# A Mamba block between two ternary feed-forward halves: fifteen states of the second token half by ScalarE and accumulating DMAs, other pieces moved, loops written out

## The reference, cut to what matters

```python
x = x + 0.5 * ffn(layernorm(x))          # ffn: x @ (ternary(W) * scale).T + bias
x = x + mamba(layernorm(x))
x = x + 0.5 * ffn(layernorm(x))

# mamba: u, z = split(x @ W_in.T); u = silu(causal conv over 4 tokens)
#        dt, B, C from u @ W_xproj.T; dt = softplus(dt @ W_dt.T + b_dt)
# for each of 16 states n, along all 4096 tokens:
h[n] = exp(dt * A[n]) * h[n] + dt * B[n] * u
y   += C[n] * h[n]
# then y = (y + u * Dskip) * silu(z); result y @ W_out.T
```

## Time and profile before

| what | us |
|---|---|
| median of 3 runs (2982.8 to 2990.77) | 2988.41 |
| the profiled execution, its own time | 2993.49 |
| its span, first to last instruction | 2991.6 |
| busy over the span: TensorE (82%) | 2457.8 |
| VectorE (83%) | 2483.3 |
| ScalarE (65%) | 1943.3 |
| GpSimd (64%) | 1921.5 |

### The profile page before, as it was taken

One profiled execution on the slowest core, in us unless ns is written; L12 is line 12 of the kernel. 1 busy time (PEld: TensorE's weight loads), 2 busy tenths in 40 slices (PEclk: granted clock), 3 DMA queues, 4 the chain that ended last, 5 costly groups with the idle time before them and its releaser, 6 DMA issues.

```text
span 2991.6 us, 42858 instructions
## 1 busy us (share of the span) xinstructions
PE 2457.8 (82%) x12448; PEld 1413.9 (47%) x12448; DVE 2483.3 (83%) x3261; ACT 1943.3 (65%) x3457; POOL 1921.5 (64%) x1705
## 2 busy tenths in 40 slices
PE   3577999899998726788889888888888888889887
PEld 1233444444443315555555555555555555555553
DVE  5565666767666649999999999999999999999991
ACT  2233766756765666677777767767777767777772
POOL 1112222222221138899989989989989989999983
PEclk8788999999998857799999999999999999999998
DMA  5454233233232263352352352353352352343330
GB/s 206 155 205 168 78 128 135 78 128 121 92 128 107 79 214 117 92 131 69 112 132 68 99 140 74 99 132 82 98 133 76 102 135 72 106 119 87 105 76 35
DMA packets 175016, 337.66 MB, mean 113 GB/s; under 512 B 41696, under 2 KB 91104, under 8 KB 174496
## 3 DMA queue, kind: packets, MB, share of 16 engines
q1 hardware_dynamic: 160928, 284.23, 28.8%
q0 software_dynamic: 13824, 50.34, 8.8%
HBM read 174.61 MB, written 109.58 MB: 95 GB/s over the span
## 4 chain that ended last, share of the span: by engine, by line
POOL 28%; DVE 13%; issue 12%; PE 5%; DMA 3%; ACT 1%; POOLq 1%; SPq 0%; DVEq 0%; ACTq 0%
POOL dbu L1055 22%; DVE h L1279 9%; DVE y L1292 3%; PE p_g L1402 2%; PE p_g L1411 1%; PE p_ht L1368 1%; POOL o L1100 1%; DMA y<-y_part 1%; POOL carry L1066 1%; POOL y L1075 1%; POOL y L1090 1%; POOL x L1094 1%; DMA dt_<-dt_scratch 1%; POOL dbu L1060 1%; DMA dtu_<-dtu_scratch 1%
## 5 line engine op out<-in xcount | busy, mean ns | idle before, releaser
L1279 DVE TENSOR_TENSOR_SCAN h<-p_da,dbu 128x512 f32<-128x512 f32 x1024 | 1189.0, 1206 | 44.7 <-ACT p_da L1161 21.9
L1055 POOL TENSOR_TENSOR dbu<-dtu_,bb 128x1024 f32<-128x1024 f32 x512 | 1205.3, 2385 | 4.7 <-DMA dtu_<-dtu_scratch 4.1
L1161 ACT ACTIVATE p_da<-dt_,neg_a 128x255 f32<-128x255 f32 x2048 | 886.5, 467 | 400.3 <-DVE h L1279 377.5
L1368 PE MATMUL p_ht<-ident,h 128*128 128x128 f32 x4096 | 596.6, 305 | 157.9 <-DVE h L1279 156.7
L1368 PEld LDWEIGHTS p_ht<-ident,h 128*128 128x128 f32 x4096 | 534.6, 159 | 250.5 <-issue 111.2
L1292 DVE SCALAR_TENSOR_TENSOR y<-p_ht,ct,y 128x1024 f32<-128x1024 f32 x400 | 505.9, 1265 | 4.9 <-PE p_ht L1368 4.8
L714 PE MATMUL p_u<-xz,wu 128*128 128x512 f16 x1536 | 351.4, 386 | 10.8 <-DVE xz L508 9.2
L1402 PE MATMUL p_g<-wo,tokt 128*128 128x512 f16 x1536 | 355.2, 389 | 1.6 <-ACT tokt L1193 1.6
L70 POOL TENSOR_TENSOR small<-small,consts 128x1 f32<-128x1 f32 x96 | 71.1, 740 | 441.4 <-DVE small L63 441.4
L1411 PE MATMUL p_g<-wz,xz 128*128 128x512 f16 x1536 | 345.2, 381 | 0.0
L363 POOL TENSOR_TENSOR late<-dt,u 128x512 f32<-128x512 f32 x64 | 81.7, 1276 | 378.0 <-DVE dt L561 378.0
(11 more groups left out here) (120 smaller groups left out, 3053.7 us busy)
## 6 DMA issues: line engine op xcount, KB each, us to landing
y<-y_part POOLq DMA_DIRECT2D x96, 512.0 KB, 5.8
bb<-b_scratch SPq DMA_DIRECT2D x128, 256.0 KB, 3.5
xin<-in_x SPq DMA_DIRECT2D x32, 512.0 KB, 5.5
x_scratch<-x SPq DMA_DIRECT2D x32, 512.0 KB, 4.8
xz_scratch<-xz SPq DMA_DIRECT2D x16, 1024.0 KB, 6.0
y_scratch<-late SPq DMA_DIRECT2D x32, 512.0 KB, 5.1
dt_scratch<-dt SPq DMA_DIRECT2D x64, 256.0 KB, 2.1
dtu_scratch<-late SPq DMA_DIRECT2D x64, 256.0 KB, 2.4
```

The lines of the kernel that those rows point to most:

```text
L1055: nc.gpsimd.tensor_tensor(state[:, 4 * f:4 * f + 4, :], dtu[:, 4 * f:4 * f + 4, :], bb[n // NB % 2][:, n % NB:n % NB + 1, :].to_broadcast( ...
L1161: ins_ = nc.scalar.activation(p_da[p % 2][:, k * T2 + 1:(k + 1) * T2], dt[:, g, 1:], ACT.Exp, scale=neg_a[:, g, n:n + 1])
L1279: nc.vector.tensor_tensor_scan(h[n % 2][:, 2 * p:2 * p + 2, :].rearrange("p g t -> p (g t)"), p_da[p % 2][:], dbu[n % 2][:, 2 * p:2 * p + ...
L1368: mm = nc.tensor.transpose(p_ht[t][:, g * P:(g + 1) * P], h[n % 2][:, g, t * P:(t + 1) * P], ident[:])
```

## The change

State parts. All states but 0 of the token half t = 1 are now written by ScalarE. State 2 goes directly to the one `y2`, the 14 others to one of three `y_part` tiles, from which GpSimd's accumulating DMAs add them three slots later: the odd ones to y itself, the even ones to y2. y2 is added to y by one more accumulating DMA.

```diff
-        y2 = [sb(f"y2_{i}", [P, D]) for i in range(2)]
-        part = [sb(f"y2_part{i}", [P, D]) for i in range(2)]
+        y2 = sb("y2", [P, D])
+        part = [sb(f"y_part{i}", [P, D]) for i in range(3)]
...
-        PARTED = (0, 5, 7, 8, 10, 11, 12)
-        SUMS = len(PARTED) - 1
+        PARTED = tuple(range(1, NS))
+        Y2_FIRST, MERGE = 2, NS
+        Y_SUM, Y2_SUM = (1, 3, 5, 7, 9, 11, 13, MERGE, 15), (4, 6, 8, 10, 12, 14)
+        SUMMED = tuple(n for n in PARTED if n != Y2_FIRST)
...
-                def add_part(c, cpar, k):
-                    wait(pool, y_added[1], c * NS + PARTED[k] + 1)
-                    wait(pool, part_added, (c * SUMS + k - 1) * 16)
-                    nc.gpsimd.tensor_tensor(small[:, 44:45], consts["minus_half"], consts["minus_half"], ALU.mult
-                                            ).then_inc(part_ready, 1)
-                    pool.wait_ge(part_ready, 1)
-                    pool.dma_start(y2[cpar][:], part[k % 2][:], accum_op=ALU.add).then_inc(part_added, 16)
+                def add_part(c, cpar, n):
+                    into, sums, done = (y[cpar][1], Y_SUM, y_summed[cpar]) if n in Y_SUM else (y2, Y2_SUM, y2_summed)
+                    wait(pool, y_added[1], c * NS + n + 1)
+                    if sums.index(n):
+                        wait(pool, *summed(c, sums[sums.index(n) - 1]))
+                    pool.dma_start(into[:], part[part_of(c, n) % 3][:], accum_op=ALU.add).then_inc(done, 16)
...
-                    nc.gpsimd.tensor_tensor(y[cpar][1][:], y[cpar][1][:], y2[cpar][:], ALU.add).then_inc(merged, 1)
+                    pool.dma_start(y[cpar][1][:], y2[:], accum_op=ALU.add).then_inc(y_summed[cpar], 16)
```

```diff
-                    nc.gpsimd.tensor_tensor(x1[t][:], x1[t][:], half_bias[:], ALU.add).then_inc(xb_done, 1)
+                    pool.dma_start(x1[t][:], dram["hb"], accum_op=ALU.add).then_inc(xb_done[t], 16)
...
+                def finish(c, t, x):
...
+                    nc.vector.scalar_tensor_tensor(out=o[x][:], in0=p_g[b][:], scalar=consts["ffn_scale"],
+                                                   in1=x1[t][:, x * HALF:(x + 1) * HALF],
                                                    op0=ALU.mult, op1=ALU.add).then_inc(g_free[b], 1)
```

Places. The units are spread anew, one slot each (a pair of `t` or `n` halves counts as one), with the last z of a chunk in slot 1 of the next body:

```diff
-        FFN = {0: [("f", 1, 0)], 1: [("f", 1, 1)]}
-        OUT = {4: [("t", 0, 0), ("t", 0, 1)], 5: [("o", 0, 0)], 6: [("o", 0, 1)], 7: [("t", 1, 0), ("t", 1, 1)],
-               8: [("o", 1, 0)], 9: [("o", 1, 1)], 10: [("n", 0, 0), ("n", 0, 1)], 13: [("f", 0, 0)],
-               14: [("f", 0, 1)], 15: [("n", 1, 0), ("n", 1, 1)]}
-        ZED = {2: [("z", 0, 0)], 3: [("z", 0, 1)], 11: [("z", 1, 0)], 12: [("z", 1, 1)]}
+        LAST = {0: [("n", 1, 0), ("n", 1, 1)], 2: [("f", 1, 0)], 3: [("f", 1, 1)]}
+        OUT = {1: [("z", 1, 1)], 4: [("t", 0, 0), ("t", 0, 1)], 6: [("o", 0, 0)], 7: [("o", 0, 1)],
+               8: [("t", 1, 0), ("t", 1, 1)], 10: [("o", 1, 0)], 11: [("o", 1, 1)], 12: [("n", 0, 0), ("n", 0, 1)],
+               14: [("f", 0, 0)], 15: [("f", 0, 1)]}
+        ZED = {5: [("z", 0, 0)], 9: [("z", 0, 1)], 13: [("z", 1, 0)]}
```

GpSimd (c_on: work for chunk i-1):

```diff
-                            if n - 3 in PARTED[1:]:
-                                add_part(i, par, PARTED.index(n - 3))
-                        if e_on:
-                            if n == 1:
-                                finish(i - 1, i - 2, 0, 1)
-                            if n == 5:
-                                add_bias(i - 2, 1)
-                            if n in (6, 7):
-                                finish(i, i - 2, 1, n - 6)
+                            if n - 3 in SUMMED:
+                                add_part(i, par, n - 3)
+                        if e_on and n == 1:
+                            add_bias(i - 2, 1)
                         if c_on:
-                            if n == 3:
+                            if n in (0, 1, 3):
+                                add_part(i - 1, 1 - par, {0: 13, 1: 14, 3: 15}[n])
+                            if n in (2, 6):
+                                gate(i - 1, 1 - par, n // 6)
+                            if n == 2:
                                 merge(i - 1, 1 - par)
-                            if n in (2, 4):
-                                gate(i - 1, 1 - par, n // 4)
```

The row scales are made in slots 10 and 14 (13 before), the first bias in 13 (12). On ScalarE tanh stands in slots 2, 6, 10 and 14 (3, 4, 12 and 13), the absolute means in 2 and 6 (2 and 4), `scale_y` in 3 and 7 (3 and 5), `high` in 0, 4, 8 and 12, `normalise` in 11 and 15; `low` takes its first half behind the first two pairs of decays of the slot after, and its second behind the other two. On VectorE:

```diff
+                            if n in (6, 10, 14):
+                                silu_part(i, n // 14, n % 6 // 4)
+                        if c_on and n == 2:
+                            silu_part(c, 1, 1)
+                        if c_on and n in (3, 7):
+                            token_scale(c, 1 - par, n // 7)
                         add_state_before(i, par, n, 0)
-                        if c_on and n in (7, 10):
-                            add_product(i, n // 10, 1)
+                        if c_on and n in (7, 8, 11, 12):
+                            add_product(c, n // 11, (n - 7) % 4)
+                        if c_on and n in (8, 12):
...
+                            row_stats(dve, nc, x1[t], stats, mv, vn, small[:, 40:41], ln_chain, stats_ready,
+                                      scale_ready, c * TT2 + t)
+                        if c_on and n == 15:
+                            finish(c, 0, 0)
+                        if e_on and n == 0:
+                            finish(i - 2, 0, 1)
+                        if e_on and n in (3, 4):
+                            finish(i - 2, 1, n - 3)
```

Loops. Both `drive` functions have no loop any more:

```diff
-            body(0, 0)
-            body(1, 1)
-            with eng.Fori(0, (C2 - 4) // 2) as turn:
-                body(turn * 2 + 2, 0)
-                body(turn * 2 + 3, 1)
-            for i in range(C2 - 2, C2 + 2):
+            for i in range(C2 + 2):
                 body(i, i % 2)
```

296 lines of the change are left out of this document (145 added, 151 removed).

## The result

The changed kernel takes **3041.1 us**, median of 4 runs (3038.7 to 3045.8), against 2989.6 of the kernel before on the same chip: a ratio of 1.0179, 95% interval 1.0158 to 1.0199. It is 1.8% slower, where the forecast was 1.7% faster. Its profiled execution has a span of 3040.7 us, 49.1 more than before.

What follows compares the result with a forecast made beforehand. VectorE was taken as the bound, slot by slot. A chunk of 110.3 us against 113.4 saves 46.5 us, the first chunk 7.0, loops 3, and the tail costs 5: 51.5 us saved, 2937 us, range 2857 to 3005.

Steps and rivals of the forecast that it cites:

- VectorE 104.1: Per chunk of the second pass: VectorE's busy time falls from 110.9 to 104.1 us, eight additions going and four finish operations coming.
- GpSimd 101.7: Per chunk: GpSimd's busy time falls from 105.5 to 101.7 us, with 11 more DMA issues at 0.90 us, 9.9 in all.
- its cover: GpSimd's products run about a slot ahead of the scans, hiding its issues while GpSimd is below VectorE, by 2.4 us.
- GpSimd busy over 107 a chunk, from issues dearer than 0.90: Sign in the changed profile that would show the forecast wrong altogether; GpSimd was expected busy 100 to 102 us.
- The merge, whose landing the prediction put only in the tail, as hidden: After the last chunk: the last sums and merge, three landings in a row, 17 us, hidden behind transposes and o units.
- TensorE 4.8 us late in three places: Per chunk: TensorE makes VectorE wait 1.7 us at slot 8, 2.3 over slots 9 to 11, 0.8 in slot 14.
- Rival 2: TensorE's units after gaps start at the lower clock, some 1 us in three places: chunk 113.3, 2982 us; chance 0.13.
- rival 1: VectorE alone is the bound, TensorE's clock stays up and it is never late: chunk 105.1, 2857 us; chance 0.25.
- First chunk, 7.0 saved: First chunk of the second pass, with none of the later work: 7.0 us saved from 105.3, bounds 9.4 and 4.
- Loops, 3 us and the rest inside 113.4: First pass's one jump back saves 3 us; second pass's jumps are already inside the 113.4 us chunk; straight code costs nothing.
- The tail, +5: After the last chunk's scans: the z unit of its second half now comes there, about 5 us more on the path.
- Rival 3: Sums land late and ScalarE waits: a loss from landings of 10.1 us; at 11 us, chunk 116.6, 3031 us; chance 0.14.

Runs made afterwards that it cites:

- a_small: Changed kernel with all part sums and the merge issued, each adding only 8 of 1,024 columns: 3005.3 us, ratio 1.0056.
- a_nosum: Changed kernel without the fourteen part sums and the merge of each chunk, ScalarE's part states kept: 2964.4 us, ratio 0.9924.
- a_8rows: Changed kernel with every part sum and the merge over only 8 of 128 partitions, whole rows: 2993.7 us, ratio 1.0018.
- a_sum14: Changed kernel with the sum of state 14 issued one slot earlier, in slot 0: 3017.6 us, ratio 1.0108.
- a_y2: Changed kernel with two y2 tiles, sums of states 13, 14, 15 in slots 0, 1, 2 and the merge in slot 4: 3011.1 us, ratio 1.0074.
- b_noloop: Kernel before the change with both loops written out, nothing else changed: 2964.2 us, ratio 0.9926.
- a_y2_warm: a_y2 with 8 further transposes on TensorE in each slot of turning units: 2996.3 us, ratio 1.0027.
- a_nosum_warm: a_nosum with 8 further transposes on TensorE in each slot of turning units: 2934.1 us, ratio 0.9820.

## Why the prediction was wrong

- **VectorE 104.1:** 105.3. The additions are as counted (272, and 240 parts on ScalarE); the price from start-to-start times was 1.2 too low, I take it because with more pauses fewer instructions overlap their neighbours, which was not tested apart.
- **GpSimd 101.7, "11 more at 0.90", and its cover:** the failed step. The busy time was right: 102.6, at 0.90 an issue. But an issue holds the queue 1.14 us, for 0.28 ahead of it and the products behind it were left out. And the cover was judged by the sum over a chunk ("as long as GpSimd is below VectorE"), where it fails slot by slot: the two dbu buffers let GpSimd run only about a slot ahead, and around the gates of slots 2 and 6 it takes 8.5 to 8.8 us and more. VectorE waits 4.8 us a chunk for it, where the sum had nothing, while GpSimd itself waits 7.0 for scans elsewhere. The issues cost 2.9 us of the 7.5 missed (a_small against a_nosum; 1.5 by a_8rows). I had named "GpSimd busy over 107 a chunk, from issues dearer than 0.90" as what would prove me wrong altogether. That sign did not show: busy is 102.6, and the 107 that it is occupied with pauses of its own was 109 before the change. It was a sign by the sum over a chunk, as blind to the slots as the cover.
- **The merge, whose landing the prediction put only in the tail, as hidden:** it is issued one slot after the sum of 14 and stands in GpSimd's queue ahead of the products. It waits in nearly every chunk, 2.8 us on average and 3.5 at most, for which the step had no term: 1.8 us of the chunk (a_sum14), 2.3 with all waits on landings (a_small, a_y2).
- **TensorE 4.8 us late in three places:** 5.7 without sums (37.4 + 13.3 over 8.9 chunks), and the places were right: 1.3 in slots 6 to 8 (I had 1.7), 2.6 in 10 to 12 (2.3), 1.7 in 14 (0.8). The slot behind a t or n slot takes 9.7 us where I took 7.7; of the rows' two cases, 8.08 and 7.22, neither was as long, because neither had as long a pause ahead of it (0.54 and 0.59 against 2.4 us). A term mis-sized by 0.9, and with the 1.2 of VectorE's work nearly the whole 2.3 us between 110.3 and 112.6. The clock fell to 0.50 behind the longer wait; behind the wait of 0.54 before the change (1819.75) it was 0.62. Rival 2 had this mechanism and nearly this price (113.3); rival 1's 105.1 did not come about even with the clock up, 110.5.
- **First chunk, 7.0 saved:** 4.9 (109.0 to 104.1 by the loads), of which b_noloop has 2.1 without any of the parts.
- **Loops, 3 us and the rest inside 113.4:** the first pass gave 6 to 7 us in these traces, over the bound of 5.6; the first dtu load of the other written-out runs comes 4 to 10 us earlier than before (1085.2 to 1091.4 against 1095.3), so one trace does not fix it. The chunk of 111.9 that was called straight code lies in the loop's first turn, ahead of its jump back; that straight code costs nothing was right all the same (112.1 in b_noloop). The written-out kernel is 22 us faster, which I had in the sum only as part of the 46.5; it did not come from the parts.
- **The tail, +5:** -5. The cause was not looked for.
- **Rival 3, ScalarE waiting for landed sums:** the sign was right and the place wrong. The median landing stayed at 5.6 us, and from 1600 to 2600 us ScalarE waited for none; GpSimd did, at the merge, where the distance was one slot. That the sign came out as in this rival is luck.
- **Range:** each rival varied one fault, and its end of 3005 held no case with two. TensorE's lateness and GpSimd's queue came together.

The sum as the runs have it: 110.3 forecast, 2.3 from TensorE's clock and VectorE's price, 2.9 from issues (by a_small), 2.3 from landings: 117.8. What stays open is how issues cost 2.9 us in a chunk in which GpSimd is idle 10; VectorE's waits place it behind the gates of slots 2 and 6, but no run spread GpSimd's work evenly to show that it then vanishes. The one attempt, the gate on VectorE, brought its own cost. The shares come from runs that each take one thing away, and add up in the order taken; with the clock up the sums cost 3.7 us a chunk without any wait of GpSimd on a landing (a_y2_warm against a_nosum_warm), not 2.9.

## What to carry to other kernels

Moving work from the busiest engine to one with room pays only if the receiving queue is free in the slots where it arrives: compare engines slot by slot, with the depth of the buffers between them, and price an issue by what it does to the distance of its neighbours, not by its own duration. Put a wait on a DMA in a compute engine's queue well behind its issue (here two slots of some 7 us did, against landings of 5.6 us in the median and 12 at most; one slot did not). And when an engine that was waited for becomes less busy, look at whoever now waits more: TensorE's clock fell behind the pauses in which it waited for VectorE, and a little useless work there was worth 30 us in the kernel without sums, 15 in a_y2, nothing in a_sum14, and cost 33 in b_noloop.
